# A two-layer recurrent block on eight cores: SyncE issues each block's input loads ahead of the previous block's stores

## The chip, the cores and the metric

The kernel runs on all 8 cores of one Trainium2 chip; core b computes sequence b of the batch. The cores exchange nothing. The metric is device time in microseconds of the slowest core for one launch.

## What is computed

The input x is 8 sequences of 4096 tokens with 1024 channels, float32. Two layers follow each other, each of the form x + s * silu(g):

```python
xn = _layernorm(x, axis=-1)
# layer 0: s
gate_x = jax.nn.sigmoid(block_diag_linear(xn, w_in, b_in))
gate_a = jax.nn.sigmoid(block_diag_linear(xn, w_a, b_a))
log_a = -gate_a * (jax.nn.softplus(a_param) + MIN_DECAY)
a = jnp.minimum(jnp.exp(log_a), 1.0 - EPS)
normed_x = xn * gate_x * jnp.sqrt(jnp.maximum(1.0 - a * a, EPS))
h, _ = closed_form_rnn_scan(normed_x, a)   # p * cumsum(x / p), p = cumprod of a
# layer 0: g, a feed-forward with ternary weights, gelu in between
x = x + h * silu(_L0_ffn_ref(xn, W1, b1, W2, b2))
# layer 1: s is a mamba2 block, g a gated feed-forward with integer weights
```

The change lies in the first stage, which computes xn and h (called s0 in the kernel) of layer 0.

## The kernel before

One program per core runs seven stages, s1 to s7, one after the other; a barrier of the core's five engines stands between two of them (`_barrier_block`). Stages hand their results on through tensors in HBM. Each stage is a function `emit_s1` ... `emit_s7` with one instruction stream per engine written out by hand. Semaphores are handled by the class `Sched`: `S.inc(..., label=...)` records the value that a semaphore has after an instruction, `S.wait(engine, label)` waits for that value, and `S.chain` also makes each instruction of VectorE (DVE) or ScalarE (ACT) wait for the one before it. In what follows b counts blocks, tt the four groups of 128 tokens in one.

Stage s1 walks over 8 blocks (NBLK) of 512 tokens. For one block:

- SyncE (SP) loads x in four transfers of 512 KB into `xtok[b % 2]` (L239), tokens on partitions. There are two such buffers.
- ACT squares them with a row sum (L327), DVE sums them (L375), and the mean and variance become the normalised `cN` (L387).
- TensorE (PE) transposes x (L279) and cN (L295) in 128x128 pieces through PSUM (`ps_tr`, two banks); DVE copies them out into `dX` (L398) and `xnT` (L410) and casts the latter to `xnbfT` (L414). `dX` is stored as xT, `xnbfT` as xnbf.
- PE multiplies by the two gates' weights (L309), ACT applies the sigmoid (L341), DVE makes log a (L422), scans it (L430), and DVE and ACT in turn compute the multiplier, 1/p and p (L348 to L361), the product and the second scan (L459). The last instruction, L469, writes h to `iL`, which is stored as s0T.

Apart from `xtok` all these tiles exist once. `dX`, `xnbfT` and `iL` are written again only after the stores of the block before have ended (waits on `s1_xTst`, `s1_xnst`, `s1_out`).

All loads and stores of s1 except the small constants leave SP's queue in program order. SP carries out its waits in that order too:

```python
for b in range(NBLK):
    # b >= 2: wait until xtok[b % 2] has been read (trx, sq, ln of block b - 2)
    # 4 loads of x for block b            -> "d"
    # wait s1_xT_done_b, 8 stores of xT   -> "o1"
    # wait s1_xnbf_done_b, 8 stores of xnbf -> "o2"
    # wait s1_h_done_b, 8 stores of s0T   -> "o3"
```

PE, ACT and DVE each wait for the four loads of block b together (semaphore "d" at 64 * (b + 1)) and then go through the block in their own order.

Of the kernel before, what the change touches and what calls it, by code (L numbers as in the profile page):

```python
# [19 lines left out]
NBLK = T // BLK  # L20
# [141 lines left out]
def emit_s1(S: Sched, env):  # L162
    nc = env.nc
    x = env.io["x"]
# [9 lines left out]
    with ExitStack() as ctx:  # L174
# [4 lines left out]
        xtok = [sb("xtok0", [128, 4096], F32), sb("xtok1", [128, 4096], F32)]  # L179
# [31 lines left out]
        @block.gpsimd  # L211
        def _(g):
            wbf3 = wbf.rearrange("p (g h j) -> p g h j", g=2, j=128)
            S.inc(g.dma_start(out=wbf3[:, 0], in_=w_in.rearrange("h i j -> i h j")),
                  "w", 16)
            S.inc(g.dma_start(out=wbf3[:, 1], in_=w_a.rearrange("h i j -> i h j")),
                  "w", 16)
            S.inc(g.dma_start(out=bcols[:, 0:8], in_=b_inT), "w", 16)
            S.inc(g.dma_start(out=bcols[:, 8:16], in_=b_aT), "w", 16)
            S.inc(g.dma_start(out=apc[:], in_=a_paramT), "w", 16)  # L220
            g.wait_ge(S.sem("w"), 80)
            S.chain(g.memset(idf[:], 1.0), "p")
            S.chain(g.affine_select(idf[:], idf[:], pattern=[[1, 128]], base=0,
                                    channel_multiplier=-1,
                                    compare_op=ALU.is_equal, fill=0.0), "p")
            S.chain(g.memset(zeros[:], 0.0), "p")
            S.chain(g.memset(Lcar[:], 0.0), "p")
            S.chain(g.memset(Scar[:], 0.0), "p")
            S.chain(g.memset(laX[:], 0.0), "p", label="s1_const")

        @block.sync
        def _(sy):
            for b in range(NBLK):
                if b >= 2:
                    S.wait(sy, f"s1_trx_{b - 2}_3_1")
                    S.wait(sy, f"s1_sq_{b - 2}")
                    S.wait(sy, f"s1_ln_{b - 2}_3")
                for tt in range(4):
                    S.inc(sy.dma_start(  # L239
                        out=xtok[b % 2][:, tt * 1024:(tt + 1) * 1024],  # L240
                        in_=x[(b * 4 + tt) * 128:(b * 4 + tt + 1) * 128, :]),
                        "d", 16)
                S.wait(sy, f"s1_xT_done_{b}")
                for k in range(NT):
                    S.inc(sy.dma_start(
                        out=xT_d[k * 128:(k + 1) * 128, b * 512:(b + 1) * 512],
                        in_=dX[:, k * 512:(k + 1) * 512]), "o1", 16,
                        label=(f"s1_xTst_{b}" if k == NT - 1 else None))
                S.wait(sy, f"s1_xnbf_done_{b}")
                for k in range(NT):  # L250
                    S.inc(sy.dma_start(
                        out=xnbf_d[k * 128:(k + 1) * 128, b * 512:(b + 1) * 512],
                        in_=xnbfT[:, k * 512:(k + 1) * 512]), "o2", 16,
                        label=(f"s1_xnst_{b}" if k == NT - 1 else None))
                S.wait(sy, f"s1_h_done_{b}")
                for k in range(NT):
                    S.inc(sy.dma_start(
                        out=s0_d[k * 128:(k + 1) * 128, b * 512:(b + 1) * 512],
                        in_=iL[:, k * 512:(k + 1) * 512]), "o3", 16,
                        label=(f"s1_out_{b}" if k == NT - 1 else None))  # L260
            sy.wait_ge(S.sem("o1"), 16 * 8 * NBLK)
            sy.wait_ge(S.sem("o2"), 16 * 8 * NBLK)
            sy.wait_ge(S.sem("o3"), 16 * 8 * NBLK)
# [1801 lines left out]
```

## Time and profile before

| | us |
|---|---|
| median of 3 runs | 6013.48 |
| the 3 runs | 5951.8, 6013.48, 6044.31 |
| the profiled execution | 5851.63 |
| its span on the slowest core (core 7) | 5850.1 |
| spans of the 8 cores | 5786.7 to 5850.1 |
| VectorE busy over the span | 2105.8 (36%) |
| TensorE busy over the span | 3871.9 (66%) |
| last instruction of DVE in s1 starts (L469), core 7 | 888.77 |

All rows are from one execution, taken by the hardware profiler on core 7 unless another core is named. The span runs from the first to the last instruction. A row of the waits gives how long an engine stood idle before a line, and what ended that: total, times, longest. In a timeline the bracket at a row's end is the idle time of the engine in front of that row and its releaser. "SPq" is SyncE's queue issuing DMAs; the duration there is that of issuing, not of the transfer.

### The profile page before, as it was taken

What the parts mean: (1) busy time and instruction counts of PE and PEld (TensorE: products, weight loads), DVE (VectorE), ACT (ScalarE), POOL (GpSimd) and SP (SyncE); (2) the same over time, 40 slices, a digit from 0 to 9 for tenths busy, and PEclk for the clock granted to TensorE, in tenths of its full rate; (3) what the DMA queues carried; (4) which work ended last, traced back from release to release, by engine and by line L of the source; (5) the groups of instructions that cost most, each with busy time, mean ns of one, the idle gap of its engine ahead of it and who ended that gap; (6) DMA issues with size and microseconds to landing.
All of it is one profiled execution on the core that took longest, in us unless ns stands there. A gap on an engine that the chain in (4) does not pass through costs nothing. (4 is left out here: it accounts for less than half of the span.)

```text
span 5850.1 us, 47991 instructions; the slowest of 8 cores (5786.7 to 5850.1 us)
## 1 busy us (share of the span) xinstructions
PE 3871.9 (66%) x16586; PEld 1770.9 (30%) x16586; DVE 2105.8 (36%) x3626; ACT 1333.8 (23%) x2162; POOL 190.8 (3%) x331
## 2 busy tenths in 40 slices
PE   1211211576859974776768777676859399996898
PEld 0100100232324431423324242332424144442344
DVE  5666667505202212335353442535322022221233
ACT  3332330222311003232333323233200011111000
POOL 0000001101010000000000000000000000001000
PEclk6555555788979995675757667575769699998899
DMA  2212217726365543010000101000056612213642
GB/s 68 72 50 79 72 50 210 199 72 196 114 201 168 191 127 77 1 43 15 29 31 13 44 1 44 15 29 29 1 144 216 144 37 72 72 37 94 222 180 108
DMA packets 295815, 521.96 MB, mean 89 GB/s; under 512 B 12928, under 2 KB 176800, under 8 KB 294560
## 3 DMA queue, kind: packets, MB, share of 16 engines
q1 hardware_dynamic: 243328, 335.57, 18.0%
q0 software_dynamic: 52256, 183.33, 11.2%
q8 instruction: 142, 2.33, 0.2%
q14 instruction: 89, 0.73, 0.0%
HBM read 358.18 MB, written 192.94 MB: 94 GB/s over the span
## 5 line engine op out<-in xcount | busy, mean ns | idle before, releaser
L676 PE MATMUL s_ps_r<-s_xnb,s_wT 128*128 128x512 bf16 x2048 | 468.3, 393 | 204.8 <-ACT s_h1s L690 161.9
L805 PE MATMUL s_ps_r<-s_h1b,s_wT 128*128 128x512 bf16 x2048 | 444.8, 381 | 66.7 <-DMA s_h1b<-h 66.7
L279 PE MATMUL s_ps_tr<-s_idf,s_xtok 128*128 128x128 f32 x256 | 59.9, 410 | 596.2 <-DMA s_xtok<-x 501.4
L1730 PE MATMUL s_ps_g<-s_xb,s_wg 128*128 128x512 bf16 x1536 | 369.1, 384 | 123.9 <-DMA s_wu<-wuT 99.5
L1855 PE MATMUL s_ps_r<-s_hgb,s_wT 128*128 128x512 bf16 x1536 | 336.0, 381 | 71.7 <-DMA s_wT<-wdT 71.7
L1736 PE MATMUL s_ps_u<-s_xb,s_wu 128*128 128x512 bf16 x1536 | 367.8, 383 | 0.0
L1712 DVE TENSOR_TENSOR s_hg<-s_sg,s_ps_u 128x512 bf16<-128x512 bf16 x192 | 132.1, 688 | 613.8 <-PE s_ps_u L1736 584.6
L676 PEld LDWEIGHTS s_ps_r<-s_xnb,s_wT 128*128 128x128 bf16 x2048 | 205.1, 101 | 466.7 <-issue 242.0
L805 PEld LDWEIGHTS s_ps_r<-s_h1b,s_wT 128*128 128x128 bf16 x2048 | 200.9, 98 | 310.6 <-issue 70.7
L690 ACT ACTIVATE s_h1s<-s_ps_r,s_b1s 128x512 bf16<-128x512 f32 x256 | 175.9, 687 | 470.3 <-PE s_ps_r L676 282.3
L1610 PE MATMUL s_ps_r<-s_yb,s_wT 128*128 128x512 bf16 x1024 | 222.7, 381 | 56.7 <-DMA s_bos<-bo_c 56.7
L787 DVE TENSOR_TENSOR s_gb<-s_s0b,s_gb 128x512 f32<-128x512 f32 x64 | 44.3, 692 | 576.7 <-ACT s_gb L825 576.7
L1752 ACT ACTIVATE s_sg<-s_ps_g 128x512 bf16<-128x512 f32 x192 | 114.6, 597 | 579.2 <-PE s_ps_g L1730 558.7
L1730 PEld LDWEIGHTS s_ps_g<-s_xb,s_wg 128*128 128x128 bf16 x1536 | 150.7, 98 | 309.9 <-issue 133.1
L1104 PE MATMUL s_ps_io<-s_winb,s_ubf 128*128 128x512 bf16 x1024 | 243.2, 380 | 0.0
L279 PEld LDWEIGHTS s_ps_tr<-s_idf,s_xtok 128*128 128x128 f32 x256 | 46.4, 213 | 610.8 <-issue 608.9
L1855 PEld LDWEIGHTS s_ps_r<-s_hgb,s_wT 128*128 128x128 bf16 x1536 | 151.2, 98 | 254.1 <-issue 76.2
L1088 PE MATMUL s_ps_io<-s_ubf,s_winb 128*128 128x512 bf16 x1024 | 223.7, 379 | 4.2 <-ACT s_zsil L1344 4.2
L1446 DVE COPY s_smallTT<-s_ps_mis 128x24 f32<-128x24 f32 x32 | 5.8, 183 | 565.4 <-PE s_ps_mis L1132 565.4
L1736 PEld LDWEIGHTS s_ps_u<-s_xb,s_wu 128*128 128x128 bf16 x1536 | 152.0, 99 | 186.6 <-issue 9.5
L1258 ACT ACTIVATE s_Mt<-s_ps_bc,s_smallTT 128x128 f32<-128x128 f32 x128 | 47.1, 368 | 593.5 <-PE s_ps_bc L1162 558.5
L1895 DVE TENSOR_TENSOR s_gb<-s_s1b,s_gb 128x512 f32<-128x512 f32 x64 | 44.3, 692 | 327.0 <-ACT s_gb L1884 240.7
(275 smaller groups left out, 5453.0 us busy)
## 6 DMA issues: line engine op xcount, KB each, us to landing
s_wf<-W1T POOLq DMA_DIRECT2D x64, 512.0 KB, 5.5
s_wf<-W2T POOLq DMA_DIRECT2D x64, 512.0 KB, 5.9
h<-s_h1s SPq DMA_DIRECT2D x8, 4096.0 KB, 19.5
s_h1b<-h SPq DMA_DIRECT2D x8, 4096.0 KB, 35.3
hgT<-s_hg SPq DMA_DIRECT2D x8, 3072.0 KB, 11.5
s_hgb<-hgT SPq DMA_DIRECT2D x8, 3072.0 KB, 19.5
s_xtok<-x SPq DMA_DIRECT2D x32, 512.0 KB, 8.9
xT<-s_dX SPq DMA_DIRECT2D x64, 256.0 KB, 3.3
```

The costliest lines, as they stand in the source:

```text
L279: ti = t.transpose(ps_tr[half][:, j * 128:(j + 1) * 128], xtok[b % 2][:, tt * 1024 + jj * 128: tt * 1024 + (jj + 1) * 128], idf[:])
L676: S.inc(t.matmul(ps[:], wT[dc][:, ft * 128:(ft + 1) * 128], xnb[b % 2][:, dc * 512:(dc + 1) * 512], start=(dc == 0), stop=(dc == 7)), "t", ...
L690: S.chain(s.activation(h1s[:, ft * 512:(ft + 1) * 512], ps[:], AF.Gelu, bias=b1s[:, ft:ft + 1]), "a", label=f"s2_gelu_{b}_{ft}")
L805: S.inc(t.matmul(ps[:], wT[fc][:, do * 128:(do + 1) * 128], h1b[b % 2][:, fc * 512:(fc + 1) * 512], start=(fc == 0), stop=(fc == 31)), "t" ...
L1088: S.inc(t.matmul(ps_io[ft % 2][:], winb[dc][:, ft * 128:(ft + 1) * 128], ubf[:, dc * 512:(dc + 1) * 512], start=(dc == 0), stop=(dc == NT ...
L1104: S.inc(t.matmul(ps_io[par][:, 0:512], ubf[:, dc * 512 + tt * 128:dc * 512 + (tt + 1) * 128], winb[dc][:, 2048 + fb * 512:2048 + (fb + 1) ...
L1610: S.inc(t.matmul(ps[:], wT[fc][:, do * 128:(do + 1) * 128], yb[b % 2][:, fc * 512:(fc + 1) * 512], start=(fc == 0), stop=(fc == 15)), "t", ...
L1712: S.chain(v.tensor_mul(hg[:, ft * 512:(ft + 1) * 512], sg[ft % 2][:], ps_u[ft % 3][:]), "v", label=f"s6_hge_{b}_{ft}")
L1730: S.inc(t.matmul(ps_g[ft % 3][:], wg[dc][:, ft * 128:(ft + 1) * 128], xb[:, dc * 512:(dc + 1) * 512], start=(dc == 0), stop=(dc == 7)), "t ...
L1736: S.inc(t.matmul(ps_u[ft % 3][:], wu[dc][:, ft * 128:(ft + 1) * 128], xb[:, dc * 512:(dc + 1) * 512], start=(dc == 0), stop=(dc == 7)), "t ...
L1752: S.chain(s.activation(sg[ft % 2][:], ps_g[ft % 3][:], AF.Silu), "a", label=f"s6_sg_{b}_{ft}")
L1855: S.inc(t.matmul(ps[:], wT[fc][:, do * 128:(do + 1) * 128], hgb[b % 2][:, fc * 512:(fc + 1) * 512], start=(fc == 0), stop=(fc == 23)), "t" ...
```

## The change

Only the instruction stream of SyncE in s1 changes. The stores of a block move into a local function `_stores(b)`, and the loop issues the loads of block b and then the stores of block b - 1. The last block's stores follow after the loop. One wait is added: before the loads of block b, SP waits until those of block b - 1 have landed. Every transfer, tile, shape and all other engines' streams stay as they are.

```diff
         @block.sync
         def _(sy):
-            for b in range(NBLK):
-                if b >= 2:
-                    S.wait(sy, f"s1_trx_{b - 2}_3_1")
-                    S.wait(sy, f"s1_sq_{b - 2}")
-                    S.wait(sy, f"s1_ln_{b - 2}_3")
-                for tt in range(4):
-                    S.inc(sy.dma_start(
-                        out=xtok[b % 2][:, tt * 1024:(tt + 1) * 1024],
-                        in_=x[(b * 4 + tt) * 128:(b * 4 + tt + 1) * 128, :]),
-                        "d", 16)
+            def _stores(b):
                 S.wait(sy, f"s1_xT_done_{b}")
                 for k in range(NT):
                     S.inc(sy.dma_start(
...
+            for b in range(NBLK):
+                if b >= 2:
+                    S.wait(sy, f"s1_trx_{b - 2}_3_1")
+                    S.wait(sy, f"s1_sq_{b - 2}")
+                    S.wait(sy, f"s1_ln_{b - 2}_3")
+                if b >= 1:
+                    S.wait(sy, f"s1_xld_{b - 1}")
+                for tt in range(4):
+                    S.inc(sy.dma_start(
+                        out=xtok[b % 2][:, tt * 1024:(tt + 1) * 1024],
+                        in_=x[(b * 4 + tt) * 128:(b * 4 + tt + 1) * 128, :]),
+                        "d", 16, label=(f"s1_xld_{b}" if tt == 3 else None))
+                if b >= 1:
+                    _stores(b - 1)
+            _stores(NBLK - 1)
```

This is SP's queue at the start of s1 before: four loads for block 0, its three groups of stores, then four loads for block 1, its stores, four loads for block 2.

```order
L239 DMA s_xtok<-x 128x1024 x4
L245 DMA xT<-s_dX 128x512 x8
L251 DMA xnbf<-s_xnbfT 128x512 x8
L257 DMA s0T<-s_iL 128x512 x8
L239 DMA s_xtok<-x 128x1024 x4
L245 DMA xT<-s_dX 128x512 x8
L251 DMA xnbf<-s_xnbfT 128x512 x8
L257 DMA s0T<-s_iL 128x512 x8
L239 DMA s_xtok<-x 128x1024 x4
```

And this is the same place in the changed program, where L260 is the load, L236, L242 and L248 are the stores.

```order
L260 DMA s_xtok<-x 128x1024 x8
L236 DMA xT<-s_dX 128x512 x8
L242 DMA xnbf<-s_xnbfT 128x512 x8
L248 DMA s0T<-s_iL 128x512 x8
L260 DMA s_xtok<-x 128x1024 x4
L236 DMA xT<-s_dX 128x512 x8
L242 DMA xnbf<-s_xnbfT 128x512 x8
L248 DMA s0T<-s_iL 128x512 x8
L260 DMA s_xtok<-x 128x1024 x4
```

Blocks 0 and 1 are now loaded at the start (eight transfers), and the four loads behind the s0T stores of block b are those of block b + 2 instead of b + 1.

## Rows read from the trace of the kernel before

**Rows 1.** The page's slices: 40 equal parts of the span, 146.25 us each.

```profile
DVE  5666667505202212335353442535322022221233
...
PEclk6555555788979995675757667575769699998899
DMA  2212217726365543010000101000056612213642
```

**Rows 2.** Windows: span, then busy times (x instructions), PEclk, DMA share, GB/s.

```profile
134.74:245.39 110.65, 21.28 (x80) 10.43 (x80) 71.71 (x63) 38.08 (x41) 0.00 (x0) 0.55 0.21 66
```

**Rows 3.** Waits of DVE, ACT and PE in s1 (0 to 960 us): total, times, longest.

```profile
DVE s_mu_c L375 <- DMA s_xtok<-x: 117.3, 7, 17.2
...
DVE s_dX L398 <- PE s_ps_tr L279: 15.1, 41, 1.0
...
DVE s_xnT L410 <- PE s_ps_tr L295: 4.0, 26, 0.2
...
ACT s_sqt L327 <- DMA s_xtok<-x: 198.1, 7, 28.7
...
PE s_ps_tr L279 <- DMA s_xtok<-x: 501.4, 7, 72.0
```

**Rows 4.** Timeline: first block's first reduction, then the second boundary, and block 2.

```profile
23.90 4.98 DVE L375 TENSOR_REDUCE s_mu_c<-s_xtok 128x1 f32<-128x1024 f32 x4
...
224.09 4.42 DVE L469 TENSOR_TENSOR s_iL<-s_eG,s_jS 128x4096 f32<-128x4096 f32 x1
228.59 4.44 SPq L257 DMA_DIRECT2D s0T<-s_iL  x8
233.24 2.53 SPq L239 DMA_DIRECT2D s_xtok<-x  x4
...
245.39 4.98 DVE L375 TENSOR_REDUCE s_mu_c<-s_xtok 128x1 f32<-128x1024 f32 x4 [16.88 <-DMA s_xtok<-x]
...
245.54 1.94 PE L279 MATMUL s_ps_tr<-s_idf,s_xtok 128*128 128x128 f32 x8 [71.72 <-DMA s_xtok<-x]
...
262.97 4.45 SPq L245 DMA_DIRECT2D xT<-s_dX  x8
...
286.10 10.52 DVE L430 TENSOR_TENSOR_SCAN s_iL<-s_laX,s_Lcar,s_zeros 128x512 f32<-128x512 f32 x8
```

**Rows 5.** Windows of the gap at that boundary, columns as in rows 2.

```profile
228.60:233.20 4.60, 0.00 (x0) 0.00 (x0) 0.00 (x0) 0.00 (x0) 0.00 (x0) 0.50 0.86 298
233.20:245.40 12.20, 0.00 (x0) 0.00 (x0) 0.01 (x1) 0.02 (x1) 0.00 (x0) 0.50 0.85 232
```

**Rows 6.** Landing times: x's loads of blocks 1 to 7, then the burst's s0T stores.

```profile
DMA to landing us min/median/max: 6.8/9.0/10.7
...
s0T<-s_iL SPq DMA_DIRECT2D x8, 256.0 KB, 4.0
```

**Rows 7.** Two reductions of one form: duration in ns, min/median/max; first and last start.

```profile
L375 DVE TENSOR_REDUCE s_mu_c<-s_xtok x32: 1219/1220/1221, 23.9 to 802.8; 128x1 f32<-128x1024 f32 x32
...
L588 DVE TENSOR_REDUCE s_red<-s_wf x32: 1219/1220/1221, 913.4 to 974.3; 128x1 f32<-128x1024 f32 x32
```

**Rows 8.** Block 1's copies and their waits for transposes; windows with the granted clock.

```profile
146.60 0.69 DVE L398 COPY s_dX<-s_ps_tr 128x512 f32<-128x512 f32 x1 [0.61 <-PE s_ps_tr L279]
147.45 0.69 DVE L398 COPY s_dX<-s_ps_tr 128x512 f32<-128x512 f32 x1 [0.16 <-PE s_ps_tr L279]
...
149.49 1.42 DVE L398 COPY s_dX<-s_ps_tr 128x512 f32<-128x512 f32 x2 [0.16 <-PE s_ps_tr L279]
...
145.38:149.40 4.02, 3.88 (x16) 2.99 (x16) 2.68 (x4) 0.00 (x0) 0.00 (x0) 0.50 0.00 0
149.44:151.10 1.66, 1.31 (x9) 0.92 (x10) 1.43 (x3) 0.00 (x0) 0.00 (x0) 1.00 0.00 0
```

**Rows 9.** Core 4: wait for x, start of s2; then core 7's start of s2.

```profile
DVE s_mu_c L375 <- DMA s_xtok<-x: 106.1, 7, 16.3
...
888.43 0.06 DVE L583 MEMSET s_acc<- 128x1 f32 x1 [7.80 <-PEq L150]
...
901.34 0.06 DVE L583 MEMSET s_acc<- 128x1 f32 x1 [8.14 <-PEq L150]
```

## Prediction

> **What bounds the kernel now.** I read the page's slices first. The change touches only stage s1, which fills about the first six of the forty slices: VectorE is the busiest compute engine there, at five to seven tenths, and TensorE's granted clock is near half for most of it [rows 1]. Next the busy times of one whole block, from one first reduction to the next. It lasts 110.65 us; DVE is busy for 71.71 of them, ACT for 38.08, PE for 21.28, and the DMA engines for a fifth [rows 2]. No engine is full, so the block is a chain, and DVE has the largest part of it. The view of waits tells what DVE stands still for: the load of x, 7 times, 117.3 us in all [rows 3]. That is 16.8 us at each of the seven boundaries between the eight blocks. PE and ACT wait for the same load (501.4 and 198.1 us), but mostly while DVE is still working, so their sums are not what a block loses.
>
> The timeline of a boundary shows why DVE waits. DVE's last instruction of the block, L469, runs from 224.09 to 228.51. Only then does SP's queue get past its wait for that result: it issues eight stores of s0T (228.59) and behind them the four loads of the next block of x (233.24). The loads are down at 245.4, when DVE, PE and ACT all start again [rows 4]. In this gap of 16.88 us no compute engine does anything [rows 5]. The loads have no need of L469: their buffer was last read a whole block earlier. They stand behind it in SP's program order only.
>
> **The change part by part.** SP now issues the loads of block b+1 before the three groups of stores of block b. Since the stores of block b-1 are already ahead of them, these loads leave SP right behind the s0T stores of block b-1, where the loads of block b stood before.
>
> *When the data comes.* Take L469's end of block b-1 as zero. The s0T stores are issued from 0.1 to 4.5 and the loads from 4.7 to 7.3, as now, and all 4.2 MB are down at 16.9 [rows 4, 5]. But the data is wanted only after block b: 110.65 - 16.88 = 93.8 us. The slack is 93.8 - 16.9 = 76.9 us; one load takes 6.8 to 10.7 us from issue to landing [rows 6], so even several times that stays hidden. The loads of block 1 are issued once those of block 0 have landed, while DVE's first reduction is at 23.90 [rows 4] and block 1's data is wanted some 90 us later.
>
> *What goes.* DVE starts L375 right behind L469: 7 x 16.8 = 117.3 us, less some 0.04 us that lie between any two neighbours, 7 x 0.04 = 0.3. I take 117.0.
>
> *What is late next.* (a) ACT's squares of the new block, which DVE needs before L379: ACT now waits 198.1 / 7 = 28.3 us for x where DVE waits 16.8, so it is free 11.5 us earlier than DVE; four squares with their reads are 4.9 us (ACT restarts with DVE and both are through after 5), so they are done before DVE asks. (b) PE's first eight transposes, 1.94 us [rows 4], go in front by some 70 us; nothing waits. (c) L430 writes over iL while the s0T stores of the block before may be on their way: it comes 286.10 - 245.39 = 40.7 us into a block, thus now 40.7 us after these stores are released; they are down by 16.9 at the latest (median landing 4.0) [rows 4, 6]. Slack 23.8 us. (d) the xT stores are released 262.97 - 245.39 = 17.6 us into a block, just behind the end of the burst; what waits for them is a block away. Each of these costs nothing as long as its slack stands; if (c) were late by 10 us at each boundary, 70 of the 117 would be gone.
>
> *The added waits.* At b >= 2 SP waits for trx, sq and ln of block b-2 and for xld of b-1: all happened a block earlier. Behind them in SP's queue are the loads and then the xT stores of b-1, which wait for DVE anyway. At b = 1 the wait for xld_0 really holds SP, until the first load lands, before PE's first transposes and DVE's 23.90; the stores behind it wait for evictions later than that. Cost nothing.
>
> *Work beside the burst.* The burst of 4.2 MB, at 298 and then 232 GB/s [rows 5], now lies beside DVE's reductions, normalisation and first copies instead of beside nothing. Before shows no such pair of instruction and SP queue load into SBUF. One end: DVE is held for the whole burst and all 117 are given back. The other: nothing. The nearest row is L588 in the next stage, a reduction of the same 128x1024 form that runs while weights stream in; it takes 1219 to 1221 ns, exactly as L375 does with idle DMA engines [rows 7]. I take nothing. The Trainium skill says the same as a rule (SBUF — State Buffer, "two separate sides"): engine ports and DMA ports are disjoint, and a queue of SP's isn't fed through the port that VectorE shares with GpSimd. By that rule the sum would be the same 117.0, and the equal durations agree with it.
>
> *TensorE's clock.* At the lower clock (0.50, 1.2 GHz) a pair of copies waits 0.61 + 0.16 = 0.77 us for its transposes, at the upper (1.00, 2.4 GHz) 0.16 [rows 8]. Per block there are 7 such pairs; they now cost (15.1 + 4.0) / 8 = 2.4 us [rows 3]. All at the lower clock would be 5.4, all at the upper 1.1. The first eight transposes no longer stand 10 us ahead of the rest, so the clock may rise a little later, if these eight count at all. Over seven blocks: from 21 us lost to 9 gained. They came after long idleness both times, and the clock rose only well into the second group, so I take 0 and keep both ends.
>
> The sum: 5851.63 - 117.0 = 5734.6 us for an execution like the profiled one (span 5850.1, 1.5 around it), span 5733.1. No other stage is touched; a barrier orders each core's stages, so s2 and all behind it start 117 us earlier. The measured runs are longer than the profiled one, median 6013.48 against 5851.63, and nothing in the trace says where the 162 us lie. Since s1 is set by DVE's fixed durations, I take the same difference off: 6013.48 - 117.0 = **5896.5 us**. That is a ratio of 0.9805, by the profiled execution 0.9800. About 2% is what a measurement of this kernel can tell from no change, and the forecast stands on that line.
>
> **The rivals.**
> *The clock stays down* through all transposes of s1: saving 117 - 21 = 96, 5917 us. For it: PE idles even longer ahead of the eviction phase. Against: the rise comes in the middle of the dense phase, which is unchanged.
>
> *The exposed load was longer in the longer runs.* If the 2.8% by which they exceed the profiled one were memory time, waits such as this would be among what grew; with waits a fifth longer the saving is 140, 5873 us. The seven waits of core 4 are 106.1 against core 7's 117.3 [rows 9], so the load does depend on what neighbours do.
>
> *DVE is held by the burst*, or the loads don't come early: no saving, 6013 us. Against it: rows 7, and the order of SP's queue, which leaves no doubt where the loads stand.
>
> *Lock-step, slower than before.* The load waits are what pulled the cores apart: core 4 starts s2 at 888.43, core 7 at 901.34 [rows 9]. Without them all eight start s2 together and hit memory together with every weight stream. Core 4, out of step, waited a tenth less per load, so full step might cost a tenth of transfer-bound time. Slices with DMA at 5 or more are 10 of 40 [rows 1], 1463 us; a tenth is 146, and 146 - 117 leaves the kernel 29 us slower, 6042 us. It decides from 8% on. Against: DVE and PE are busy through much of those slices, and only two cores are out of step now, so little is left to align. The Trainium skill's HBM Reference ("Specifications") gives each of two cores that stream together about 358 GB/s, more than the stretches of rows 5 reach; by that page lock-step would cost nothing, and no row here shows two cores at their common limit.
>
> **How the numbers follow.** Forecast (saving 105 to 128) 0.76; clock 0.07; longer waits, larger saving 0.09; no saving 0.03; lock-step 0.05, of which 0.02 beyond 2%. The line of 2% is 120.3 us against 6013. The runs shown spread from 5951.8 to 6044.31, so a median of a few moves by half a per cent or more, and the forecast's 0.76 splits into 0.36 above the line and 0.40 below. With the 0.09: faster by over 2% 0.45; within 2% 0.53; slower 0.02. Range: the saving alone gives 5873 to 5917; the runs' own spread below and above their median, -62 to +31, and the 162 us down to the profiled execution, partly, widen it to 5790 to 5965.
>
> **What would show it.** Right: DVE's wait for x at L375 is gone for all seven blocks, blocks start 93.8 us apart, L583 starts near 784, and L375 still takes 1.22 us beside the burst. The SP queue shows loads behind s0T as before, but eight loads at the start. Wrong: a DVE wait at L379 for ACT or at L430 for the s0T stores, L375 longer than 1.22, more than 5 us per block of waits of L398 and L410 for PE, or the lead of 117 us at 784 lost again by the end through longer weight waits.

## The result and the profile after

| | before | changed |
|---|---|---|
| median of all runs, us | 5927.97 (10 runs) | 5734.84 (10 runs) |
| profiled execution, us | 5851.63 | 5731.38 |
| its span, slowest core | 5850.1 (core 7) | 5729.8 (core 3) |
| s2 begins, over the cores | 888.8 to 902.6 | 783.8 to 785.8 |

The ratio of the compared executions is 0.9764, 95% interval 0.9718 to 0.981: the changed kernel is faster, but since the interval reaches past 0.98, this comparison doesn't settle whether by more than 2%. In part of the executions of either kernel one die or both run at a lower granted clock and take some per cent longer; the ratio leaves those out, and by their times all three runs shown ahead of the prediction (5951.8 to 6044.31, against 5834.5 to 5904.14 for the executions of the kernel before that are compared) were such ones.

The views of the changed kernel are of core 3, its slowest; its lines from L260 on are those of before plus 6 (L375 is now L381, L469 is L475). First the page's slices, to be read against [rows 1].

```profile
DVE  6777768134012213534334353533412022221233
...
PEclk7555557888799967575665757576679699997999
DMA  3131247355466540001010000100065621214653
```

Stage s1 now ends in the sixth slice instead of early in the seventh, and VectorE's share in its slices has risen from five or six tenths to six or seven (the 7 and the 8 in the seventh slices are mostly s2). The waits of DVE, ACT and PE between 0 and 860 us, to be read against [rows 3]:

```profile
DVE s_dX L404 <- PE s_ps_tr L285: 14.1, 38, 1.0
...
DVE s_xnT L416 <- PE s_ps_tr L301: 3.2, 21, 0.2
...
ACT s_rs_c L338 <- DVE s_rs_c L389: 90.9, 8, 12.9
...
PE s_ps_tr L285 <- DVE s_dX L404: 458.1, 11, 63.9
```

Behind the first block no engine waits for x any more: DVE's 117.3 us are gone without a successor. PE's idle time has a new name, not a new cost: it was booked on the load (501.4) and is now booked on the first eviction (458.1), for PE is free from the gates to the next block's evictions either way. The same holds for ACT: it has its squares done early and then waits for the variance. The timeline of the second boundary and the windows of one block and of the burst, to be read against [rows 2, 4, 5]:

```profile
204.45 1.06 ACT L333 ACTIVATE s_sqt<-s_xtok 128x1024 f32<-128x1024 f32 x1
...
207.96 4.43 DVE L475 TENSOR_TENSOR s_iL<-s_eG,s_jS 128x4096 f32<-128x4096 f32 x1
...
212.42 4.98 DVE L381 TENSOR_REDUCE s_mu_c<-s_xtok 128x1 f32<-128x1024 f32 x4
...
212.46 4.44 SPq L248 DMA_DIRECT2D s0T<-s_iL  x8
217.18 3.03 SPq L260 DMA_DIRECT2D s_xtok<-x  x4
...
229.50 4.49 SPq L236 DMA_DIRECT2D xT<-s_dX  x8
...
252.90 10.52 DVE L436 TENSOR_TENSOR_SCAN s_iL<-s_laX,s_Lcar,s_zeros 128x512 f32<-128x512 f32 x8
...
118.33:212.42 94.09, 21.33 (x80) 11.15 (x80) 71.72 (x64) 38.15 (x40) 0.00 (x0) 0.57 0.25 78
212.40:229.00 16.60, 5.42 (x26) 4.15 (x27) 13.91 (x20) 0.41 (x2) 0.00 (x0) 0.55 0.91 250
```

The reduction L381 has no bracket: it starts 0.03 us after L475's end at 212.39. The stores and loads leave SP as soon behind DVE's last instruction as before, and 250 GB/s move for 16.6 us, but DVE is busy for 13.91 us of that time. A block lasts 94.09 us instead of 110.65, with the same 71.7 us of DVE work. The reduction hasn't grown beside the burst [rows 7]:

```profile
L381 DVE TENSOR_REDUCE s_mu_c<-s_xtok x32: 1220/1220/1221, 24.6 to 686.1; 128x1 f32<-128x1024 f32 x32
```

### The profile page after: what moved, and what is told of

Same layout as the page of the kernel before. It is cut to its first block and busy times, and to the rows that moved or that the text cites. A ratio compares the mean times of both kernels' runs of the same rounds, so it can differ in the third digit from the quotient of the medians.

```text
span 5729.8 us, 47998 instructions; the slowest of 8 cores (5669.5 to 5729.8 us)
## 1 busy us (share of the span) xinstructions
PE 3867.2 (67%) x16586; PEld 1769.7 (31%) x16586; DVE 2105.5 (37%) x3626; ACT 1337.6 (23%) x2162; POOL 191.6 (3%) x331
## 5 line engine op out<-in xcount | busy, mean ns | idle before, releaser
L682 PE MATMUL s_ps_r<-s_xnb,s_wT 128*128 128x512 bf16 x2048 | 466.6, 392 | 194.3 <-ACT s_h1s L696 151.7
L285 PE MATMUL s_ps_tr<-s_idf,s_xtok 128*128 128x128 f32 x256 | 58.6, 403 | 481.9 <-DVE s_dX L404 458.1
L1861 PEld LDWEIGHTS s_ps_r<-s_hgb,s_wT 128*128 128x128 bf16 x1536 | 151.7, 99 | 258.6 <-issue 86.9
L1742 PEld LDWEIGHTS s_ps_u<-s_xb,s_wu 128*128 128x128 bf16 x1536 | 151.7, 99 | 185.5 <-issue 7.8
## 6 DMA issues: line engine op xcount, KB each, us to landing
h<-s_h1s SPq DMA_DIRECT2D x8, 4096.0 KB, 19.7
```

What stands on the lines that cost most here:

```text
L285: ti = t.transpose(ps_tr[half][:, j * 128:(j + 1) * 128], xtok[b % 2][:, tt * 1024 + jj * 128: tt * 1024 + (jj + 1) * 128], idf[:])
L682: S.inc(t.matmul(ps[:], wT[dc][:, ft * 128:(ft + 1) * 128], xnb[b % 2][:, dc * 512:(dc + 1) * 512], start=(dc == 0), stop=(dc == 7)), "t", ...
L1742: S.inc(t.matmul(ps_u[ft % 3][:], wu[dc][:, ft * 128:(ft + 1) * 128], xb[:, dc * 512:(dc + 1) * 512], start=(dc == 0), stop=(dc == 7)), "t ...
L1861: S.inc(t.matmul(ps[:], wT[fc][:, do * 128:(do + 1) * 128], hgb[b % 2][:, fc * 512:(fc + 1) * 512], start=(fc == 0), stop=(fc == 23)), "t" ...
```

## The experiments

Two yardsticks are used throughout. *Start of s2* is the start of GpSimd's first DMA of that stage, averaged over the eight cores of the profiled execution; it is 899.2 and 900.9 for two executions of the kernel before (mean 900.0) and 784.9 for the changed kernel. *Mean span* is the span averaged over the four cores of a die, over all dies of all runs whose four granted clocks were above 0.742; its standard deviation between dies is 5 to 17 us, so that a difference of two such means is good to some 3 to 7 us (one standard error), and the limit of 0.742 is a choice: one of 0.746 would lower the mean of the changed kernel by 2 us.

### e1: only every second boundary

```diff
-            for b in range(NBLK):
-                _loads(b)
-                if b >= 1:
-                    _stores(b - 1)
-            _stores(NBLK - 1)
+            for b in range(0, NBLK, 2):
+                _loads(b)
+                _loads(b + 1)
+                _stores(b)
+                _stores(b + 1)
```

Here and below `_loads(b)` stands for the changed kernel's waits and four loads of block b.

> Loads run ahead at every second boundary only: those into blocks 1, 3, 5 and 7 are hidden, those into 2, 4 and 6 stay behind the s0T stores. Theory A (a boundary costs its 16.8 us wait and nothing else changes): DVE waits for x three times, about 50 us in all, s2 starts at 901 - 67 = 834, the kernel is 67 us faster than before, ratio 0.989. Theory B (lock-step of the cores, or another effect that comes with the prefetch as a whole, gives part of the gain or takes it): the saving is not proportional; s2 starts near 834 all the same but the rest of the kernel differs from before by more than 10 us.

DVE's timeline has the wait at block 2 and none at block 3:

```profile
229.01 4.98 DVE L383 TENSOR_REDUCE s_mu_c<-s_xtok 128x1 f32<-128x1024 f32 x4 [17.35 <-DMA s_xtok<-x]
323.27 4.98 DVE L383 TENSOR_REDUCE s_mu_c<-s_xtok 128x1 f32<-128x1024 f32 x4
```

DVE waits 50.8 us in 3 waits; s2 starts at 835.2, 64.8 us earlier than before. Mean span 5739.2 (7 dies) against 5804.0 (26 dies of before in the same job): 64.8 us less. Only two of the seven executions can be compared (5757.0 and 5764.7 us, against 5819.3 to 5849.7 for ten of before), so there is no interval. The saving is the same at each boundary, 64.8 / 4 = 16.2 us: theory A.

### e2: loads ahead of the s0T stores, but still behind L469

```diff
                 S.wait(sy, f"s1_h_done_{b}")
+                if b < NBLK - 1:
+                    _loads(b + 1)
                 for k in range(NT):
                     S.inc(sy.dma_start(
                         out=s0_d[k * 128:(k + 1) * 128, b * 512:(b + 1) * 512],
...
```

Here and in e3 the four loads at the head of the loop are left out, and `_loads(0)` stands ahead of it.

> The loads of the next block still wait for L469 but are issued ahead of the eight s0T stores instead of behind them. Theory A (the 16.9 us are transfer and issue time of stores and loads together, one behind the other): the stores' share goes (4.6 us of issue and most of their 2 MB), the wait at a boundary falls from 16.8 to 9 or 11 us, saving 7 x 6 to 7 x 8 = 42 to 56 us, ratio about 0.992. Theory B (the loads' own latency makes the gap, the stores ahead cost little): the wait stays above 14 us and less than 20 us are saved.

```profile
DVE s_mu_c L383 <- DMA s_xtok<-x: 73.5, 7, 11.5
```

That is 10.5 us per boundary instead of 16.8: without the eight stores ahead of them the loads cost 10.5, and those stores had added 6.3. s2 starts at 852.8, 47.2 us earlier. The ratio is 0.9933 (0.9876 to 0.999); mean span 5749.6 (12 dies), 54.4 us less. Theory A. The kernel as a whole gained 7 us more than s1 did; e4 will show that two sets of runs of one program differ by 3.4.

### e3: loads in the middle of the block

```diff
+                if b < NBLK - 1:
+                    _loads(b + 1)
                 S.wait(sy, f"s1_h_done_{b}")
```

> The loads of block b+1 are issued in the middle of block b, behind the xnbf stores and ahead of the wait for L469, so no s0T store stands beside them; they have some 68 us until they are wanted. Theory A (any place that is early enough hides them fully): no DVE wait for x, s2 starts near 784, the same time as the changed kernel, ratio to before 0.976 to 0.980. Theory B (the position of the burst matters, beside the reductions in the changed kernel, beside gates and scans here): a difference of more than 5 us in s1.

No wait of DVE for x; s2 starts at 784.5, 0.4 us from the changed kernel. The ratio is 0.9843 (0.9792 to 0.9895) from three executions, above the 0.976 to 0.980 that theory A gave for it; the mean span is 5699.7 (7 dies), 104.3 less than before, and the changed kernel's own, from the runs of the result, is 5699.1 (19 dies). The place of the burst doesn't matter: theory A for s1. But e3 saves 115.5 us in s1 and 104 in all.

### e4: the kernel before against itself

> The kernel before against itself. It shows what two sets of runs of one program differ by. Theory A (saving is 117 us, the rest of the measured 0.9764 is spread of the runs): ratio within 0.995 to 1.005, but single medians spread by 20 us or more. Theory B (the change saves some 20 to 30 us beyond s1): the ratio here is within 0.2% of 1 with a narrow interval.

Ratio 1.0028 (0.9986 to 1.007); mean span 5800.6 (12 dies) against 5804.0. Two sets of runs of one program thus differ by 0.3% with an interval of 0.4% to either side. The ratio lies within theory A's 0.995 to 1.005 and outside the 0.2% of theory B, but its interval is too wide to exclude B. A ratio such as 0.9764 can overstate the gain by some tenths of a per cent.

### e5: every load twice

```diff
                 if b >= 1:
                     S.wait(sy, f"s1_xld_{b - 1}")
+                    for tt in range(4):
+                        S.inc(sy.dma_start(
+                            out=xtok[b % 2][:, tt * 1024:(tt + 1) * 1024],
+                            in_=x[(b * 4 + tt) * 128:(b * 4 + tt + 1) * 128, :]),
+                            "q", 16)
+                    sy.wait_ge(S.sem("q"), 64 * b)
```

> The changed kernel, in which every load of x for blocks 1 to 7 is done twice: a first copy into the same buffer, a wait for it, then the real one. At a boundary 6.2 MB instead of 4.2 MB move beside DVE's reductions, normalisation and copies. Theory A (DVE and ACT aren't slowed by the burst and the slack of 77 us covers it): no DVE wait for x, L381 stays at 1220 ns, s2 starts at 784 to 786. Theory B (the burst beside the engines has a price that the one burst already pays in part): L381 or the copies grow, or s2 starts later than 790.

SP's queue at the second boundary, a window over what it moves, and the reduction (L387 here):

```profile
217.06 2.45 SPq L260 DMA_DIRECT2D s_xtok<-x  x4
229.00 2.98 SPq L266 DMA_DIRECT2D s_xtok<-x  x4
232.09 4.82 SPq L236 DMA_DIRECT2D xT<-s_dX  x8
...
212.50:240.00 27.50, 11.17 (x58) 7.38 (x58) 21.96 (x29) 1.57 (x3) 0.00 (x0) 0.69 0.84 243
...
L387 DVE TENSOR_REDUCE s_mu_c<-s_xtok x32: 1219/1220/1221, 24.6 to 685.9; 128x1 f32<-128x1024 f32 x32
```

243 GB/s run for 27.5 us beside reductions, normalisation, copies and transposes, the xT stores are pushed back by some 3 us, and s2 starts at 785.0. The normalisation (812 ns) and the copies into `dX` (691 ns) have kept their durations too, against 812 and 692 in the changed kernel. The ratio is 0.9825 (0.9778 to 0.9873), the mean span 5700.2 (6 dies). The traffic beside the engines is free here: theory A.

### e6: the changed kernel again

> The changed kernel once more, on the chip of these runs. Theory A (117 us saved in s1, some 10 us given back in s2, where neighbouring cores that start in step spend 740 to 760 us instead of 730): ratio 0.979 to 0.984, and s1 ends at 784 on all cores. Theory B (the change really saves 140 us as the first ratio 0.9764 says): ratio below 0.978.

Ratio 0.982 (0.9767 to 0.9872), s2 starts at 784.6; mean span 5697.6 (10 dies) against 5800.2 (14 dies) of before: 102.6 us less. The ratio is within theory A's 0.979 to 0.984, although its interval reaches below 0.978. The ratio rests on two of its eight executions.

### e7 and e8: the h1 store of s2 in quarters, with and without the change

In s2 ACT writes h1 of a block into one tile, SP stores it in one transfer of 4 MB, and ACT may start on the next block only when that has landed. Of PE's waits in s2 of the changed kernel (785 to 1542 us) the one that goes back to this store is the largest:

```profile
PE s_ps_r L682 <- ACT s_h1s L696: 151.7, 7, 43.7
PE s_ps_s L654 <- DVE s_acc L596: 139.5, 1, 139.5
```

```diff
+            def _h1st(b):
+                for q in range(4):
+                    S.wait(sy, f"s2_gelu_{b}_{8 * q + 7}")
+                    S.inc(sy.dma_start(
+                        out=h1_d.rearrange("(f p) t -> p f t", p=128)[:, 8 * q:8 * q + 8, b * 512:(b + 1) * 512],
+                        in_=h1s.rearrange("p (f c) -> p f c", c=512)[:, 8 * q:8 * q + 8, :]),
+                        f"h{q}", 16, label=f"s2_h1st_{b}_{q}")
...
-                    S.wait(sy, f"s2_h1done_{b - 1}")
-                    S.inc(sy.dma_start(
-                        out=h1_d.rearrange("(f p) t -> p f t", p=128)[:, :, (b - 1) * 512:b * 512],
-                        in_=h1s.rearrange("p (f c) -> p f c", c=512)),
-                        "o1", 16, label=f"s2_h1st_{b - 1}")
+                    _h1st(b - 1)
...
-                if b > 0:
-                    S.wait(s, f"s2_h1st_{b - 1}")
                 for ft in range(32):
+                    if b > 0 and ft % 8 == 0:
+                        S.wait(s, f"s2_h1st_{b - 1}_{ft // 8}")
```

> The changed kernel, and in s2 the store of h1 (4 MB per block, for which ACT and then PE stand still) goes in four quarters, each released as soon as its eight activations are done and waited for by its own eight of the next block. Theory A (the time given back in s2 sits in that store's exposed end, where two neighbours in step share the memory): PE's wait for ACT in s2 falls from 150 us to below 40, s2 falls to 590 to 640 us and its spread over the cores to a few us; the kernel is at 0.955 to 0.962 of before. Theory B (s2's spread comes from its weight loads): the wait falls, but the spread of s2 between pairs of cores stays at 20 us or more.

> The kernel before with the same quarter stores in s2, the change in s1 left out. Theory A (in step or not makes no difference once the h1 store is hidden): s2 as short as in the run with both, and the difference between the two kernels is the full 115 to 118 us of s1, instead of some 105. Theory B (the given-back time sits elsewhere): the difference between the two stays near 105 us.

All of PE's waits in s2 of e7 (core 7, 785 to 1370 us):

```profile
PE s_ps_s L654 <- DVE s_acc L596: 138.1, 1, 138.1
PE s_ps_r L682 <- DVE s_wT L617: 39.9, 3, 24.7
PE s_ps_r L682 <- DVE s_acc L620: 8.7, 1, 8.7
PE s_ps_c L658 <- DVE s_sc L603: 0.9, 1, 0.9
```

The wait for ACT has vanished. s2 lasts 579.9 us on average (576.7 to 582.1 over the cores) instead of 739.7 (726.5 to 756.6). That is 10 us below the 590 to 640 that theory A of e7 gave, and more than the wait itself; the spread between the cores went with it, as theory A said. e7's ratio to the kernel before is 0.9543 (0.9488 to 0.9598), just under theory A's 0.955 to 0.962, e8's 0.9716 (0.9687 to 0.9745). e7 beats both kernels of the study.

Theory A of e8, that its distance to e7 would be the full gain of s1, fell, and theory B holds. Mean spans are 5644.4 (e8, 11 dies) and 5543.4 (e7, 9 dies), 101.0 apart, while s1 differs by 114.4. With that store hidden, some 13 us are still missing.

### e9: loads from GpSimd's queue

```diff
         @block.gpsimd
         def _(g):
+            _loads(0)
...
+            for b in range(1, NBLK):
+                _loads(b)
...
         @block.sync
         def _(sy):
             for b in range(NBLK):
-                if b >= 2:
-                    S.wait(sy, f"s1_trx_{b - 2}_3_1")
...
```

`_loads` has the changed kernel's waits, issued by GpSimd; SP keeps only the stores, in the order of before.

> The order of SP's stores as before, but the loads of x leave GpSimd's queue, which waits for nothing of DVE's last result: it issues the loads of block b+2 as soon as block b's buffer has been read. Theory A (the loads stood behind L469 by SP's program order alone): DVE's wait for x is gone for all seven blocks, s2 starts within 5 us of 784 and the time is that of the changed kernel, ratio 0.978 to 0.984. Theory B (GpSimd's issuing needs something that VectorE holds while it copies or scans): loads are issued late, single waits of some us at L375's place, or DVE's instructions grow; s2 starts at 790 or later. The wait for constants at the start may move by some us, since GpSimd issues four loads ahead of them.

```profile
22.04 2.16 POOL L221 DMA_DIRECT2D s_xtok<-x  x4
41.90 2.09 POOL L221 DMA_DIRECT2D s_xtok<-x  x4 [17.71 <-DVE s_dX L404]
135.68 2.09 POOL L221 DMA_DIRECT2D s_xtok<-x  x4 [91.68 <-PE s_ps_tr L301]
```

The loads of block 2 leave at 41.90, right after block 0's last transposes of x and their evictions; DVE waits for x nowhere, and s2 starts at 785.3. Mean span 5694.5 (7 dies) against 5798.4 (7 dies) of before. Three executions, 5707.9, 5731.9 and 5732.2 us, can be compared with one of before, 5805.4, so the ratio that theory A gave isn't tested. For s1 it is theory A: with e3, which stays in SP's queue and only goes ahead of the wait for L469, it shows that the loads were late because they stood behind that wait.

## Why the prediction was right or wrong

**The time, 5896.5 us with a range of 5790 to 5965: wrong.** The changed kernel's median is 5734.84, below the range. The step that failed is "I take the same difference off: 6013.48 - 117.0". What it had wrong is the first term of that sum, the level of 6013.48 us, and not the difference. None of the three runs behind it had come down to the profiled execution's 5851.63, while six of the changed kernel's ten lie at 5714.25 to 5738.3. The other sum of the same text, made against the profiled execution (5851.63 - 117.0 = 5734.6), is within 0.3 us of the measured median. That is partly luck: the slowest core before was 7 and spent 766 us in s2, the slowest after is 3 and spent 756. The text said that nothing in the trace tells where the 162 us between the two lie, and it chose the median nevertheless. The three runs left no trace, but e6's profiled execution, which took 5962.5 us, shows where such time can lie: on its die 0, at granted clocks of 0.713 to 0.72, s1 takes 784.5 to 785.0 us as elsewhere, but s6 takes 836 to 912 us against 798 to 801 on die 1, s4 2162 to 2168 against 2117 to 2121, on cores 0 and 1 s7 takes 536 and 550 against 469 to 477, and on cores 2 and 3 s2 takes 796 and 787 against 733 to 763, with excesses of 33 to 50 us in s3 and s5. The windows of core 1 and of core 5, on the other die, over the same 100 us of s6 (4700 to 4800 us; the columns are those of rows 2):

```profile
4700.00:4800.00 100.00, 96.48 (x364) 39.60 (x362) 17.63 (x24) 13.73 (x23) 0.00 (x0) 0.80 0.16 53
```

```profile
4700.00:4800.00 100.00, 96.51 (x449) 43.58 (x447) 21.57 (x29) 16.69 (x28) 0.00 (x0) 1.00 0.16 53
```

Both TensorEs are busy for 96.5 us, but one, at a granted clock of 0.80, gets 364 matmuls done where the other does 449. In this execution the extra time is TensorE's and lies behind s1. The rival of longer waits falls too. e4's profiled execution, the kernel before at 5885.65 us, has cores 6 and 7 at a clock of 0.736 and 0.737: their DVE waits 118.9 and 117.1 us for x, against 113.4 to 117.3 on the six others, while their s6 takes 822 and 815 us against 797 to 801 and their s7 524 and 519 against 470 to 476. The range should have reached down to the profiled execution less the saving; the text weighed that end "partly".

**The saving in s1: right.** Predicted 117.0 on core 7, measured 901.7 - 784.2 = 117.5 there, and 114.3 on the mean of the cores, since cores 4 and 5 had waited less (106.1 and 111.1). The boundaries are 94.1 us apart (said: 93.8), and s2 starts at 784 as said. The step "the data comes at 16.9 and is wanted at 93.8" holds: for block 2, e3 issues the loads 24 us later than the changed kernel does (147.45 instead of 123.09) and e9 81 us earlier (41.90), and neither changes s1. One reading of the text was off: in the six slices of s1 VectorE is at five or six tenths [rows 1], and the 7 belongs to s2; no term of the sum used it.

**What is late next: nothing, right in each point.** (a) ACT's squares end at 205.6, 6.8 us ahead of DVE's first reduction. (b) PE's transposes cost nothing. (c) L436 comes 40.5 us into the block, no wait. (d) the xT stores leave SP at 229.50, half a microsecond behind the end of the burst. In e5, where the burst runs on, they are pushed back by some 3 us, and no engine waits for them.

**Work beside the burst: taken as nothing, right**, with 1220 ns beside 250 GB/s and, in e5, beside 243 GB/s for 27.5 us. The rule of the Trainium skill (SBUF — State Buffer, "two separate sides") that was quoted for it agrees with both traces.

**TensorE's clock: taken as nothing, right.** The waits of the copies for PE went from 19.1 to 17.3 us, a gain of 2 within the stated -21 to +9. The windows show 0.57 instead of 0.55 as granted clock of a block.

**Lock-step: a small loss is there, a tenth of the size priced, and its mechanism isn't shown.** The prediction gave it 146 us if real, which would have turned the sign. Measured is that the cores now start s2 within 2.0 us of each other, and that 115 us saved in s1 end as 103 (e3, e5, e6 and e9, each against the kernel before in its own job: 104, 100, 103, 104). The profiled pair of the result alone doesn't show the loss: averaged over the eight cores, its spans fall by 113.7 us (5810.6 to 5697.0). e1, whose neighbours start s2 0.6 to 1.7 us apart, saved 65 of 65, and e2, which leaves neighbours 5 to 7 us apart, 54 of 47. Against standard errors of 3 to 7 us the four losses of 11 to 15 us together are clear of noise; e2's extra 7, beside the 3.4 of e4, hardly is. In the profiled executions, over all pairs of neighbours at the usual clock (0 and 1, 2 and 3, and so on) of the kernels with the whole h1 store, s2 lasts 745.1 us on average where a pair starts it up to 0.5 us apart (14 pairs), 737.8 us at 0.6 to 2.3 us (14 pairs), and 728.9 us at 5 us or more (6 pairs), with standard errors of 2 to 3 us. In five of these executions the two slowest cores are partners, at 756 to 766 us (2 and 3 of the changed kernel, 6 and 7 of the kernel before), but other partners differ by up to 13 us. The Trainium skill (HBM Reference, "Specifications") says that two cores share one memory domain; that fits the slow pairs. But its share of about 358 GB/s per core lies above what they moved (283 and 294 GB/s on cores 3 and 2 of the changed kernel from 971 to 1018 us, in their longest wait for the store, with their DMA engines 0.99 busy), and by it being in step would cost nothing, which these durations speak against if the distance is what sets them. That shared memory is the cause is argued, not shown: no run changed the distance of two neighbours alone. A part of the store's time comes from its own core in any case: of the 18.0 MB that core 3 moved from 965 to 1030 us, 12.7 went through GpSimd's queue, which streams the weights W2T, and the 4 MB took 47.0 us to land, against a median of 19.7 for the eight stores. e7 and e8 show that the h1 store's exposed end carries the spread between cores, but not the whole 13 us: in those two profiled executions the kernel with the change is slower by 4.5 us in s2 and by 1.5 to 3.3 us in each of the five later stages. Where that comes from stays open.

**The chances.** "Faster by over 2%" had 0.45 and "within 2%" 0.53. The first comparison gave 0.9764, the second, e6, 0.982, and the mean spans give 103 of 5802 us, 1.8%. Neither interval (0.9718 to 0.981, 0.9767 to 0.9872) lies wholly on one side of 0.98. The first ratio was large on the side of before: its compared executions reach up to 5904 us, those of the later job with e1 to e4 lie between 5819 and 5850, while the changed kernel's agree in the result and in e6 (5708 to 5738 and, from two executions, 5717 to 5733). So the forecast ratio of 0.980 was as good as these runs can tell.

## What to carry to other kernels

A queue that both loads and stores is a chain: a load behind a store that waits for the last result is as late as that result, however many buffers there are. Issue loads ahead of the stores of the block being computed, or from a queue that waits for nothing, and read the gain off the wait of the engine that has the most work, not off those with the largest wait sums. Predict a difference against an execution whose stages and clock are known, and widen the range to the level of that execution; a median of few runs may be that of executions at a lower clock, as 6013.48 against 5851.63 seems to have been here. After such a fix, look for the next single buffer whose whole store stands between two blocks: here it was worth 156 us, more than the change itself.

## What was not expected

Hiding h1's store gave more than its visible wait. PE waited 151.7 us for ACT on the slowest core (127 to 152 over the cores), but s2 fell by 160 us on average, and with it its spread from 30 to 5 us. The windows over s2 of core 3, first of the changed kernel, then of e7, show a second part (columns as in rows 2):

```profile
785.00:1541.40 756.40, 467.63 (x2056) 205.64 (x2056) 286.00 (x362) 177.69 (x257) 89.75 (x162) 0.81 0.53 156
...
785.30:1367.10 581.80, 452.74 (x2056) 203.01 (x2056) 286.20 (x362) 177.16 (x257) 88.31 (x162) 0.88 0.69 203
```

On this core s2 fell by 174.6 us. 151.7 are PE's wait. Another 14.9 are in the same 2056 matmuls, which take 452.74 us instead of 467.63: in the changed kernel the granted clock stood at 0.50 (1.2 GHz) in the wait from 980 to 1010 us, and over the whole stage it is 0.81, against 0.88 in e7, which has no such waits. A third part is the last store, of which only a quarter is left to wait for: from ACT's last result to GpSimd's first DMA of s3 it takes 6.0 us instead of 16.5. The three make 177.1; DVE's first sum in s2 came 2.5 us later (142.0 instead of 139.5).

The saved time didn't all arrive at the end. Exposed loads had pulled the cores 14 us apart at the end of s1 in one profiled execution and 6 us in another; without them they arrive within 3 us. About a tenth of the saved time is spent again later, in pieces of a few microseconds, in stages that weren't touched. That the closer start is the reason isn't shown.
